# Linear attention: expert rows gathered one a half step, the next weights loaded in ten pieces

## The reference

```python
x = x + tanh(g_xattn[0]) * softmax_attention(layernorm(x), ctx)
x = x + tanh(g_ffn[0]) * experts_top2(layernorm(x))         # sum of 2 gated expert rows for each token
q, k, v = heads(layernorm(x), Wq), heads(ctx, Wk), heads(ctx, Wv)
q1, k1 = relu(q @ Wqf.T), relu(k @ Wkf.T) * mask             # 64 features a head
kv, k_sum = sum_n k1[n] v[n].T, sum_n k1[n]                  # per sequence and head
x = x + tanh(g_xattn[1]) * ((q1 @ kv) / (q1 @ k_sum + 1e-8) @ Wo.T + bo)
x = x + tanh(g_ffn[1]) * attention_and_experts(x)            # weights ca_w first
```

## Time and profile before

| what | value |
|---|---|
| median of three executions | 2604.84 us |
| span of the profiled execution, first to last instruction | 2704.4 us |
| TensorE matmul busy | 2250.3 us, 83% |
| VectorE busy | 1841.5 us, 68% |
| ScalarE busy | 1152.8 us, 43% |
| POOL busy | 1105.8 us, 41% |
| mean granted TensorE clock | 0.907 of 2.4 GHz |
| mean DMA rate | 116 GB/s |

### The profile page before, as it was taken

The page is one execution under the profiler, slowest core; times in us unless marked ns, Lnnn a source line. Parts: engine busy times, 40 slices in busy tenths (PEclk is TensorE's granted clock), DMA queues, the critical chain, the costliest instruction groups (busy, mean ns, idle before and its releaser), DMA issues. The chain is left out here.

```text
span 2704.4 us, 60407 instructions
## 1 busy us (share of the span) xinstructions
PE 2250.3 (83%) x20880; PEld 1699.7 (63%) x20880; DVE 1841.5 (68%) x3965; ACT 1152.8 (43%) x2509; POOL 1105.8 (41%) x1111
## 2 busy tenths in 40 slices
PE   6889989786878579994799899899888699998890
PEld 4555555443766357773677777787766577886670
DVE  4888888762547567775878878878876365444654
ACT  2777667554434223332344444444333354332230
POOL 2455555554144400001445445455577301325526
PEclk9898899765889689997999999999999799999995
DMA  5555455433358431211332332332334462445644
GB/s 115 125 134 141 121 137 131 113 114 100 104 178 277 133 130 52 64 31 51 82 83 62 81 85 59 81 87 57 85 100 135 134 206 90 142 148 167 200 153 144
DMA packets 249859, 313.10 MB, mean 116 GB/s; under 512 B 45152, under 2 KB 202848, under 8 KB 249056
## 3 DMA queue, kind: packets, MB, share of 16 engines
q1 hardware_dynamic: 188592, 219.11, 28.9%
q0 software_dynamic: 26624, 58.79, 7.9%
q10 hardware_dynamic: 34352, 31.34, 3.4%
HBM read 122.40 MB, written 102.24 MB: 83 GB/s over the span
## 5 line engine op out<-in xcount | busy, mean ns | idle before, releaser
L2119 POOL TENSOR_TENSOR ca_qk<-ca_qk,ca_q_swap 128x512 f32<-128x512 f32 x160 | 249.9, 1562 | 371.2 <-DVE ca_q_swap L2297 369.6
L735 DVE TENSOR_REDUCE soft_top<-soft_pa 128x2 fp32r<-128x512 f32 x512 | 328.4, 683 | 99.6 <-PE soft_pa L816 81.8
L630 ACT ACTIVATE soft_prob<-soft_pb 128x512 f32<-128x512 f32 x512 | 286.0, 594 | 191.8 <-PE soft_pb L809 171.9
L809 PE MATMUL soft_pb<-soft_rep 32*128 32x256 f32 x1024 | 213.4, 368 | 62.1 <-DVE soft_top L735 39.6
L809 PEld LDWEIGHTS soft_pb<-soft_rep 32*128 32x128 f32 x1024 | 140.1, 218 | 181.8 <-issue 85.8
L1440 PE MATMUL moe_pgu<-moe_w_hi,moe_xt_hi 128*128 x472 | 198.1, 420 | 39.8 <-DVE moe_xt_lo L1357 24.9
L816 PE MATMUL soft_pa<-soft_rep 31*128 31x256 f32 x1024 | 223.0, 375 | 6.0 <-DVE soft_top L735 3.5
L1459 PE MATMUL moe_py<-moe_w_d,moe_at 128*128 x788 | 219.1, 394 | 1.7 <-issue 0.8
L1363 DVE TENSOR_TENSOR moe_act_f<-moe_silu,moe_pgu 128x256 f32<-128x256 f32 (+1 forms) x236 | 88.5, 375 | 165.4 <-ACT moe_silu L1258 111.2
L2389 PE MATMUL ca_py<-ca_w_hi,ca_ot_hi 128*128 128x256 f32 x512 | 154.4, 302 | 33.1 <-DVE ca_ot_lo L2318 32.8
L1258 ACT ACTIVATE moe_silu<-moe_pgu 128x256 f32<-128x256 f32 (+1 forms) x236 | 82.1, 348 | 230.0 <-PE moe_pgu L1440 149.8
(11 more groups left out here) (377 smaller groups left out, 6384.7 us busy)
## 6 DMA issues: line engine op xcount, KB each, us to landing
ca_q_swap<-ca_q_f SPq DMA_DIRECT2D x640, 64.0 KB
moe_xs<-moe_rows SPq DMA_DIRECT2D x236, 128.0 KB
soft_rep<-soft_parts SPq DMA_DIRECT2D x378, 64.0 KB
moe_rows<-soft_blank SPq DMA_DIRECT2D x27, 768.0 KB
moe_ys_rows<-moe_ys ACTq DMA_DIRECT2D x134, 128.0 KB
moe_ys<-moe_ys ACTq DMA_DIRECT2D x102, 128.0 KB
moe_xd<-scratch SPq DMA_DIRECT2D x64, 128.0 KB
ca_vs<-ca_v SPq DMA_DIRECT2D x32, 256.0 KB
```

What stands on the lines that cost most here:

```text
L630: act.activation(prob[:, k % 4, h, :], p_b[:, 2 * T * h:2 * T * (h + 1)], ACT.Exp).then_inc(prob_ready, 1)
L735: dve.tensor_reduce(heads[:, j, :, g], p_a[:, 2 * T * h:2 * T * (h + 1)].rearrange("p (c s) -> p c s", c=HALF), AX, ALU.max).then_inc(a_do ...
L809: mm = pe.matmul(p_b[:, out], rep[of, i % 4, g, at:at + PART], rep[of, i % 4, g, 0:T], start=True, stop=True)
L2119: pool.tensor_tensor(qk[:, u % 2, m, :], qk[:, u % 2, m, :], q_swap[:, p % 2, :], ALU.add).then_inc(qk_ready, 1)
```

## The change

`late_tile(half)` turns a half step's number into a tile: half steps 13, 15, 17 and so on to 43 give 0 to 15, all others none. VectorE makes the sum of that tile there, and SP stores it two half steps later (`half - 2`). POOL makes one gather for each `kf` that VectorE has made (`kf_ready`), which starts in half step 8; `root(1)` goes ahead of all gathers and the others between them. VectorE waits for the `ys` rows (`written`) in chunk -1, tile step 2. The weights in `held_w` come in ten pieces of 1024 columns: 0 and 1 in chunk 3 after `wlo_ready`, 2 to 5 in chunk 5 after `landed(31)`, 6 to 9 in chunk 6.

```diff
--- before.py
+++ after.py
@@ -1054,6 +1054,11 @@
             linear = LinearAttention(ahead, st)
         LATE = FIRST[1]
 
+        def late_tile(half):
+
+            n, rest = divmod(half - 2 * LinearEarly.TPC - 5, TOP)
+            return n if n >= 0 and rest == 0 else None
+
         def written(eng, blocks):
 
             for i in range(3):
@@ -1152,14 +1157,14 @@
                     if t not in [combined_behind(b - LOAD_LAG) for b in range(ALL)] and t + SUMS < TILES:
                         load_sum(t + SUMS)
                 def last_sum(n):
-                    t = LATE + n
-                    if t < TILES:
+                    if n is not None and LATE + n < TILES:
+                        t = LATE + n
                         store_sum(t)
                         if t + SUMS < TILES:
                             load_sum(t + SUMS)
 
                 if then is not None:
-                    linear.sync(sp, last_sum, landed)
+                    linear.sync(sp, lambda half: last_sum(late_tile(half - 2)), landed)
                 else:
                     for n in range(COUNT[1]):
                         last_sum(n)
@@ -1193,13 +1198,13 @@
                 if then is not None:
                     ahead.root(pool, 0)
                     written(pool, ALL)
-                    for t in tiles_of(1):
-                        for k in range(TOP):
-                            gather(t, k)
-                        if t == LATE + 6:
-                            ahead.root(pool, 1)
-                    for n in range(2, CHUNKS):
-                        ahead.root(pool, n)
+                    ahead.root(pool, 1)
+                    for n in range(max(TOP * COUNT[1], 2 * TILES)):
+                        if n % (2 * ahead.TPC) == 2 * ahead.TPC - 2 and n // (2 * ahead.TPC) + 2 < CHUNKS:
+                            ahead.root(pool, n // (2 * ahead.TPC) + 2)
+                        if n < TOP * COUNT[1]:
+                            pool.wait_ge(linear.kf_ready, n + 1)
+                            gather(LATE + n // TOP, n % TOP)
                     return
                 pool.wait_ge(until_ready, 1)
                 early = list(tiles_of(1))[:HELD]
@@ -1378,7 +1383,12 @@
                         ahead.normalise(dve, 0)
 
                 if then is not None:
-                    linear.vector(dve, lambda n: combine(LATE + n) if LATE + n < TILES else None)
+                    def late_sum(half):
+                        n = late_tile(half)
+                        if n is not None and LATE + n < TILES:
+                            combine(LATE + n)
+
+                    linear.vector(dve, late_sum, lambda: written(dve, ALL))
                     return
                 for n in range(ALL - 3, ALL):
                     dve.wait_ge(ys_out[n % 3], 16 * (n // 3 + 1))
@@ -1643,15 +1653,12 @@
 
         TRANSPOSE, QK, QF = (1, TPC, 1), (5, 4, 2), (0, PAIRS, 2)
         PAIR_AT = (0, 2, 1, 3, 4, 6, 5, 7)
+        NEXT = 10
         steps = [Tile(0, n) for n in range(-1, CHUNKS + 1)]
 
         def sync(sp, beside, landed):
 
             for ch in steps:
-                if ch.n == 1:
-                    landed(TILES - 1)
-                    for at in range(0, HELD_W, HELD_W // 4):
-                        sp.dma_start(held_w[:, at:at + HELD_W // 4], c["ca_w"][:, at:at + HELD_W // 4]).then_inc(next_in, 16)
                 after = ch.plus(2)
                 if live(after) and after.c >= 2:
                     sp.wait_ge(t_ready, TPC * (ch.n + 1))
@@ -1661,6 +1668,14 @@
                 for t in range(TPC):
                     for half in range(2):
                         beside(2 * (TPC * (ch.n + 1) + t) + half)
+                    piece = {1: 0, 3: 1}.get(t) if ch.n == 3 else TPC * (ch.n - 5) + t + 2
+                    if piece is not None and 0 <= piece < NEXT and ch.n in (3, 5, 6):
+                        if piece == 0:
+                            sp.wait_ge(wlo_ready, early.PIECES)
+                        if piece == 2:
+                            landed(TILES - 1)
+                        at = slice(piece * HELD_W // NEXT, (piece + 1) * HELD_W // NEXT)
+                        sp.dma_start(held_w[:, at], c["ca_w"][:, at]).then_inc(next_in, 16)
                     r = Row(ch, t - 4)
                     if r.live:
                         for n in range(0 if r.n == 0 else r.n + 1, min(r.n + 2, TILES)):
@@ -1669,7 +1684,7 @@
                         sp.dma_start(x_out[r.n], xo[:, r.slot, :]).then_inc(stored[r.slot], 16)
             for s in range(2):
                 sp.wait_ge(stored[s], 16 * TILES // 2)
-            sp.wait_ge(next_in, 16 * 4)
+            sp.wait_ge(next_in, 16 * NEXT)
 
         def scalar(act, finished):
             act.wait_ge(const_in, 16 * 6)
@@ -1707,7 +1722,7 @@
                         past(act, y_mm, r.n - 1)
                         act.activation(o_t[:, r.slot, :], p_y[:, 0:DIM], ACT.Copy).then_inc(ot_ready, 1)
 
-        def vector(dve, beside):
+        def vector(dve, beside, finished):
             dve.wait_ge(const_in, 16 * 6)
             dve.wait_ge(gate_ready, 1)
             dve.wait_ge(zeroed, 5)
@@ -1716,6 +1731,8 @@
                 new = ch.plus(1)
                 for t in range(TPC):
                     now, r1, r2, r4 = Row(ch, t), Row(ch, t - 1), Row(ch, t - 2), Row(ch, t - 4)
+                    if ch.n == -1 and t == 2:
+                        finished()
                     for half in range(2):
                         if now.live:
                             dve.wait_ge(kf_mm, 2 * now.n + half + 1)
@@ -1897,7 +1914,7 @@
                             mm = pe.transpose(p_y[:, k * PART:(k + 1) * PART],
                                               on[:, r3.slot, k * PART:(k + 1) * PART], ident[:])
                         mm.then_inc(ot_mm, 1)
-        self.sync, self.scalar, self.vector, self.tensor = sync, scalar, vector, tensor
+        self.sync, self.scalar, self.vector, self.tensor, self.kf_ready = sync, scalar, vector, tensor, kf_ready
 
 
 def _layout_linear_attention(a):
```

## The result

The changed kernel takes 2578.09 us (2569.92 to 2583.23, four runs) against 2604.24 of the kernel before beside it (2599.87 to 2608.91): ratio 0.9891, 95% interval 0.9853 to 0.9929, 26.15 us less. The forecast was 2581.9, 22.9 less, in a range of 2566 to 2593. Both kernels were measured once more, 2570.05 against 2605.61, ratio 0.9861 (0.9834 to 0.9887). By these intervals the gain is 18 to 38 us in the first comparison and 29 to 43 in the second.

A forecast was written before the change was run, and what follows sets the result against it. TensorE bounds the steady linear-attention chunk, the stage being slow only at its beginning. Gains of 7.0 (A), 4 (B) and 12.9 (C) less 1 (D) make 22.9 us: 2604.84 to 2581.9 us, range 2566 to 2593.

The forecast's parts named there:

- the likeliest case: Whole kernel: forecast of 2582 us, gains of 18 to 28 us, given chance 0.50.
- Part A: Linear attention's prologue: moving gathers and sums out of half steps 0 to 7 gains 7.0 us, bounds 5 and 8.
- Part B: Late releases in POOL's gather burst: spacing gathers out removes them, 4 us in timed runs, bounds 0 and 16.
- Part C: Long chunk of 49.64 us: loading the next weights in ten later pieces gains 12.9 us, bounds 10 and 16.2.
- Part D: Half steps 13 to 43: sixteen sums beside a full TensorE cost 1 us together, bounds 0 and 15.5.
- what is late next is the chain product, `qk_hi`, `qk_lo`, which stays: Prologue, after the first transpositions: the product chain stays as it is once sums and gather waits leave; no separate size.
- The first (B in full): Gather-burst lags are in the timed runs in full, 16 us: gain 34.9, 2570 us; chance 0.25.
- The second: Lags follow the gathers to their new places and sums delay `kf`: gain 10 to 15, about 2592 us; chance 0.16.
- third: VectorE becomes the bound in steps 13 to 43, sums ahead of the next `kf`: slower, 2616 us; chance 0.04.
- Its threshold: Steps 13 to 43: slower once each sum with its two gathers costs TensorE more than 1.2 us.
- The fourth: Waits on gather and `xr` hide others that end as late, so no gain: 2604 us; chance 0.05.
- no "remote": Trace sign: no release marked "remote", one that no semaphore explains, of some us after 881.

The follow-up runs named there:

- e_burst24: Changed kernel with gathers not paced by kf_ready: 24 back to back, then root(2), the other eight as sums free slots; 2578.55 us, ratio 0.9872 to the kernel before.
- e_sums: Changed kernel with its gathers and sums, but the next weights loaded in one go at the start of chunk 6; 2577.10 us, ratio 0.9902 to the kernel before.
- e_xrfirst: Kernel before, with only the first two xr row loads put ahead of the 5.2 MB load at chunk 1; 2577.56 us, ratio 0.9879 to the kernel before.
- e_dve2: Changed kernel plus two more sum-sized VectorE instructions after each odd half step 13 to 43; 2575.95 us, ratio 0.9902 to the kernel before.
- e_before: Kernel before, unchanged, profiled once more; one execution of 2611.88 us, trace span 2610.1 us.
- e_dve4: Changed kernel plus four more sum-sized VectorE instructions after each odd half step 13 to 43; 2592.77 us, ratio 0.9948 to the kernel before.
- e_pieces: Kernel before with only the next weights' load changed to ten pieces, gathers and sums as before; 2588.61 us, ratio 0.9944 to the kernel before.
- e_onego2: Kernel before with its one 5.2 MB load moved from the start of chunk 1 to that of chunk 2; 2588.34 us, ratio 0.9942 to the kernel before.
- e_burst: Changed kernel without POOL's wait on kf_ready; roots between held the gathers to groups of six and eight; 2576.64 us, ratio 0.9897 to the kernel before.

## Why the prediction was right, and where its terms were off

The direction, the places and the likeliest case were right. The gain of 26.1 us in the stage is 3.2 more than forecast, by four terms that were off in both directions: A gave 4.0 more than forecast, B 4 less, C 2.2 more and the sums of D cost 1 less. That the total came so near is in part luck, since 4 of the 22.9 us were put on something that gave nothing.

*Part A, 7.0 forecast.* The clean pair of traces gives 17.57 - 9.58 = 8.0 us to the first query product, the upper of my bounds. The prologue gains 10.2 (30.7 to 20.5). The step that failed is "what is late next is the chain product, `qk_hi`, `qk_lo`, which stays": sums stood in that chain too, and its part, from the first query product to the first `kf`, went from 13.1 to 10.9 us, of which 1.9 are the two sums between the last `qk_lo` and the first `kf`. The five half steps behind gave 0.8 more.

*Part B, 4 forecast, 0 to 16 bounded.* It measured 0. The late releases were real in the trace, where they cost 338.1 - 321.7 = 16.4 us of the stage (12.8 to 16 by my working), and absent from a second trace of the same kernel; e_burst24 shows no such delay beside a burst of 24 either. I had read the 99.6 us between span and median as time that recording adds. It was an unusual execution, and the lags in the earlier trace rows were no price for anything. What was still right was to doubt them because of that difference. Which thing delayed that execution no run here shows.

*Part C, 12.9 forecast.* It measured 15.1 (50.5 to 35.4). I compared the long chunk with a steady one of 36.7, but this one, with less output work, needs 35.4 when nothing stalls. That was in the working as a bound, the 16.2 us wait, and not in the value. The mechanism was only half right: I named the transfer, and the traces of e_sums and e_xrfirst show that it is the rows of `xr` asked for behind it with no lead. I also left out the 1 MB of chunk 3's rows that stands between the two. The cost of a piece, nothing, was right (no wait of `xo` over 1 us in the changed kernel).

*Part D, 1 forecast.* It measured 0: the three chunks behind chunk 1's start, which have four sums each, are 36.73 us. The sums raise VectorE's busy time from 28.65 to 32.06, which leaves 4.7 us of the chunk, and e_dve2 took 2.8 of these at 0.2 us a chunk.

Together: 10.2 + 0.8 + 15.1 = 26.1.

*The rivals.* The first (B in full) fell with e_before. The second and third (sums delay `kf`) fell with the steady 36.7 us chunks; e_dve4 shows the third as it would be, at three times the added load: 16.4 us of stage lost. Its threshold was wrong: the sums cost nothing with VectorE busy 87% of the chunk, and two more instructions next to nothing at 94%. The fourth fell with the prologue's 20.5 us and the `xo` that no longer waits. By the Trainium skill's rule on two SBUF inputs (SBUF — State Buffer, "Who interferes with whom") D would have been up to 16 us; the gathers took 997 to 1076 ns beside the sums, and the same with 64 more such instructions, so it isn't seen here. (The 1.26 us that the prediction gives as the longest of the 32 gathers is the longest of all 80 in the earlier trace rows; the 32 of that trace reach 1.23.) The Trainium skill's fixed 2.0 us (DMA: Bandwidth & Descriptors, "Anatomy of one DMA") is given there for transfers that GpSimd issues, and as latency to completion for the most part; that I multiplied it by six as time on SP's queue was a misreading. In the runs the six more transfers cost nothing: e_pieces and e_xrfirst have the same stage.

*What the trace was to show.* First query product 9.6 us after the first transposition (10.5 forecast; the 892 itself held only for a trace in which the stage starts at 881.74), no `xr` wait, no "remote", and chunks of 36.7 but for chunk 1's start, which at 35.4 lies 1.3 us under: three signs came whole and one nearly.

## What to carry to other kernels

Before a large load goes onto a queue, ask which small load behind it is wanted next, and whether it has a lead: in the traces two 128 KB loads put ahead were worth the same 15 us as splitting and moving 5.2 MB. Work off the path is free beside a full engine only as long as its own engine's total fits (here up to 94% busy), and it should not stand in a start-up where each step waits for the last. Hold a profile's span against the timed runs first; if it is 4% longer, record again before a number is taken from it.

## What the runs showed of the hardware

Two traces of the same kernel had spans of 2704.4 and 2610.1 us. The first has releases 4 to 14 us late that no instruction explains, those looked at all beside bursts of indirect gathers; the same bursts in the second trace had none. Of the 94.3 us between the two traces 30.9 came before the stage, 16.4 in it and 47.0 behind it.

5.2 MB in four transfers with one row behind them took 14.6 us to that row's landing (e_sums). With 6.2 MB ahead of it, the issue of the next transfer itself held SP for 8.13 us (e_xrfirst) and 6.78 (e_onego2), where the one behind the 5.2 MB of e_sums took 0.65.

An indirect gather took POOL 1.00 us in the median when it went by itself, in a burst of 24 and beside VectorE at 94%; the longest took 1.25 (e_burst).
